# Where the last outputs of the first attention stand among the second's first score rounds, and idle products at two borders

## The reference

```
x = x + attn0(layernorm(x))                  # 16 heads of 64, linear attention, causal, phi = elu + 1
x = x + xattn0(layernorm(x), ctx, mask)      # 16 heads of 16, softmax over 375 context rows, no projections of q, k, v
x = x + ffn0(layernorm(x))                   # own causal attention ("third attention" here), then four experts
x = x + attn1(layernorm(x))                  # causal attention through a rank of 64
x = x + xattn1(layernorm(x), ctx)            # window of 64 rows, rotary
x = x + ffn1(layernorm(x))                   # ternary weights
```

## Time and profile before

| | before |
|---|---|
| median of 3 runs | 1294.95 us |
| profiled execution | 1293.48 us |
| its span, first to last instruction | 1291.7 us |
| mean granted clock of TensorE | 0.991 |
| TensorE busy | 1247.5 us (97%) |
| VectorE busy | 734.2 us (57%) |
| ScalarE busy | 503.1 us (39%) |
| GpSimd busy | 281.4 us (22%) |
| chain that ended last, share on TensorE | 92% |

### The profile page before, as it was taken

How to read it: one execution, slowest core, us unless ns; L and a number is a source line. 1 busy time by engine, 2 the same in 40 slices (tenths; PEclk the granted TensorE clock), 3 DMA queues, 4 the chain that set the end, 5 groups by cost and what they waited for, 6 DMA issues and landing times.

```text
span 1291.7 us, 34601 instructions
## 1 busy us (share of the span) xinstructions
PE 1247.5 (97%) x14031; PEld 969.1 (75%) x14031; DVE 734.2 (57%) x1730; ACT 503.1 (39%) x1075; POOL 281.4 (22%) x382
## 2 busy tenths in 40 slices
PE   7999999999999999899989999999999899999996
PEld 5788777785667666666667999999999677777765
DVE  5666666666666676478764211111112656789987
ACT  2111111120555555556656323323332454444444
POOL 2000000101211111688844000000001000224532
PEclk9999999998999999899999999999999999999999
DMA  7212211101422221012201100000000000000002
GB/s 226 64 45 46 45 31 33 33 20 31 89 68 65 64 61 31 8 48 81 73 16 44 30 1 0 0 3 0 0 1 1 3 7 4 14 19 18 15 11 59
DMA packets 48480, 45.38 MB, mean 35 GB/s; under 512 B 15408, under 2 KB 44896, under 8 KB 48336
## 3 DMA queue, kind: packets, MB, share of 16 engines
q1 hardware_dynamic: 47824, 42.87, 12.7%
q10 hardware_dynamic: 512, 0.46, 0.1%
HBM read 39.44 MB, written 2.78 MB: 33 GB/s over the span
## 4 chain that ended last, share of the span: by engine, by line
PE 92%; issue 2%; DVE 2%; ACT 2%; DMA 1%; SPq 1%; POOL 0%; ACTq 0%; DVEq 0%
PE banks L323 51%; PE banks L831 6%; PE banks L809 4%; PE banks L996 4%; PE banks L316 3%; PE banks L1009 3%; PE banks L847 3%; PE banks L1058 3%; PE banks L970 3%; PE banks L660 2%; PE banks L618 2%; PE banks L1037 2%; ACT area L1571 1%; PE banks L1053 1%; PE banks L900 1%
## 5 line engine op out<-in xcount | busy, mean ns | idle before, releaser
L1856 DVE TENSOR_REDUCE Y_room<-banks 112x2 f32<-112x750 f32 x128 | 114.1, 934 | 46.9 <-PE banks L809 46.7
L2004 DVE TENSOR_REDUCE area<-banks 112x8 f32<-112x896 f32 x96 | 100.1, 1084 | 56.1 <-PE banks L996 56.1
L1571 ACT ACTIVATE area<-banks 112x896 f32<-112x896 f32 x96 | 82.8, 914 | 111.2 <-PE banks L1058 111.2
L323 PE MATMUL banks<-room,area 128*112 128x256 f32 (+1 forms) x384 | 118.9, 460 | 0.3 <-ACT Y_room L1448 0.3
L2136 DVE SCALAR_TENSOR_TENSOR X<-banks,area,X 128x192 f32 (+1 forms) x56 | 23.3, 417 | 160.4 <-PE banks L323 160.2
L1649 ACT ACTIVATE room<-banks 128x256 f32<-128x256 f32 x123 | 47.2, 384 | 166.0 <-PE banks L323 165.9
L323 PE MATMUL banks<-area,room 128*128 128x224 f32 x512 | 102.6, 360 | 0.6 <-ACT area L1415 0.6
L1458 ACT ACTIVATE area<-banks,Y_room 125x896 f32<-125x896 f32 x96 | 90.1, 1010 | 32.1 <-PE banks L831 31.4
L323 PE MATMUL banks<-room,l 128*128 128x256 f32 x448 | 99.5, 379 | 0.0
L323 PEld LDWEIGHTS banks<-area,room 128*128 128x128 f32 x512 | 97.1, 193 | 3.1 <-ACT area L1415 1.0
L1303 POOL TENSOR_TENSOR rstd<-mv,kcol 112x1 f32<-112x1 f32 x48 | 9.5, 197 | 400.3 <-DVE mv L1979 400.3
(11 more groups left out here) (237 smaller groups left out, 2419.2 us busy)
## 6 DMA issues: line engine op xcount, KB each, us to landing
area<-den_scratch SPq DMA_DIRECT2D x32, 224.0 KB, 3.6
Y_room<-in_ctx SPq DMA_DIRECT2D x16, 375.0 KB
area<-in_ctxT SPq DMA_DIRECT2D x64, 93.8 KB
area<-area SPq DMA_DIRECT2D x192, 2.6 KB
l<-in_l SPq DMA_DIRECT2D x2, 1024.0 KB, 5.4
room<-in_ctxT SPq DMA_DIRECT2D x16, 112.0 KB, 2.1
X<-in_x SPq DMA_DIRECT2D x1, 1568.0 KB, 17.8
out<-X SPq DMA_DIRECT2D x12, 112.0 KB, 2.0
```

The costliest lines, as they stand in the source:

```text
L323: last = nc.tensor.matmul(dst, a, w, start=(k == 0), stop=(k == len(lhs) - 1))
L1571: a_.activation(c_pT[:, i * 8 * S:(i + 1) * 8 * S].rearrange("p (j n) -> p j n", j=2), banks[0:S, 2 + 2 * i:4 + 2 * i, 0:4 * S], ACT.Exp). ...
L1856: v_.tensor_reduce(b_nb[u][:, 4 * a + k:4 * a + k + H + 1:H], banks[0:S, 2 * x:2 * x + 2, 0:SC], AX_X, ALU.max, negate=True).then_inc(Bs[" ...
L2004: v_.tensor_reduce(c_nb[:, 8 * i:8 * i + 8].rearrange("q (j n) -> q j n", j=2), banks[0:S, 2 + 2 * i:4 + 2 * i, 0:4 * S].rearrange("q j (n ...
```

## The change

In `bank_pairs()`, round 0 of batch 1 takes the pairs longest unused, as the others do. `output_a` takes a part of its eight products, and for the last batch writes bank 6 instead of bank 7 (`residual_a` reads it there). On TensorE, `weighted_a(15)` stands in front of round 1, `output_a(14)` between rounds 1 and 2, four idle products behind `queries_b(0)`, three behind round 3. The first half of `output_a(15)` and `maxima_t(0)` stand in front of round 0 of batch 1, the second half behind it, without the wait for ScalarE's copy of the maxima. The idle products behind round 2 of batch 0 and rounds 0 and 1 of batch 1 go. On VectorE, `residual_a(14)` and the statistics of batch 2 stand behind the maxima of round 1, `normalised(15)` in front of those of round 3. At the second border idle products stand behind `output_b(14)` (3), `sums_t(15)` (3), `output_t(15)` (2) and `to_columns(0)` (3), all into bank 5.

```diff
--- before.py
+++ after.py
@@ -176,7 +176,7 @@
     for b in range(B + 1):
         for what, n in [("s", n) for n in range(3)] + [("t", n) for n in range(3)] + [("s", 3)] + [("t", n) for n in range(3, 6)]:
             if what == "s" and on(b):
-                x, y = (0, 1) if b == 0 or (b, n) == (1, 0) else sorted(range(3), key=lambda i: since[i])[0:2]
+                x, y = (0, 1) if b == 0 else sorted(range(3), key=lambda i: since[i])[0:2]
                 pairs["s", b, n] = [claim(x, ("nb", 8 * b + 2 * n + 1)), claim(y, ("nb", 8 * b + 2 * n + 2))]
             m = b - 1
             if what == "t" and on(m):
@@ -619,15 +619,20 @@
                                          a_at[:, h * S:(h + 1) * S], start=True, stop=True, tile_position=(0, LD * e))
                 last.then_inc(A["nd"].sem, 1)
 
-            def output_a(b):
-
-                pe.wait_ge(A["nm"].sem, A["nm"].at(2 * b + 2))
-                pe.wait_ge(A["xu"].sem, A["xu"].at(b))
-                pe.wait_ge(A["xte"].sem, A["xte"].at(min(b // 2 + 2, B // 2)))
-                if b == 0:
-                    pe.wait_ge(ld["a3"].sem, 16)
-                products(pb[7][0:S, 0:D], [a_oT[:, m * S:(m + 1) * S] for m in range(8)],
-                         [wo0[:, m, :] for m in range(8)]).then_inc(A["wd"].sem, 1)
+            def output_a(b, lo=0, hi=8):
+
+                if lo == 0:
+                    pe.wait_ge(A["nm"].sem, A["nm"].at(2 * b + 2))
+                    pe.wait_ge(A["xu"].sem, A["xu"].at(b))
+                    pe.wait_ge(A["xte"].sem, A["xte"].at(min(b // 2 + 2, B // 2)))
+                    if b == 0:
+                        pe.wait_ge(ld["a3"].sem, 16)
+                    if b == B - 1:
+                        pe.wait_ge(pre["b6"].sem, 1)
+                for m in range(lo, hi):
+                    last = T3.matmul(pb[6 if b == B - 1 else 7][0:S, 0:D], a_oT[:, m * S:(m + 1) * S], wo0[:, m, :], start=(m == 0), stop=(m == 7))
+                if hi == 8:
+                    last.then_inc(A["wd"].sem, 1)
 
             def phase_a(p):
 
@@ -753,12 +758,13 @@
                 last.then_inc(Bs["ut"].sem, 1)
 
             def phase_b(b, w, quarter):
+                if b == 1:
+                    output_a(B - 1, 0, 4)
+                    maxima_t(0, 0)
                 if on(b):
                     scores_b(b, 0, w, quarter)
                 if b == 1:
-                    maxima_t(0, 0)
-                    pe.wait_ge(Bs["me"].sem, Bs["me"].at(1))
-                    output_a(B - 1)
+                    output_a(B - 1, 4, 8)
                 if on(b - 2):
                     weighted(b - 2, 0, w % 2)
                     weighted(b - 2, 1, w % 2)
@@ -809,10 +815,7 @@
                     last = T3.matmul(pb[2 * x + r % 2][0:S, 0:SC], b_q[w][o:o + HD + 2, k, r % 2, :], b_ctx[w][o:o + HD + 2, k, 0:SC],
                                      start=True, stop=True)
                 last.then_inc(Bs["sg"].sem, 1)
-                if b == 0 and k > 1:
-                    pe.wait_ge(pre["b6"].sem, 1)
-                    keep_busy(6, 3)
-                if b == 1 and k < 2:
+                if (b, k) == (0, 3):
                     keep_busy(6, 3)
 
             def turned(b, n, w):
@@ -857,11 +860,13 @@
             pe.wait_ge(pre["masks"].sem, 1)
             scores_b(0, 0, 0, 0)
             sums_a(B - 1)
-            output_a(B - 2)
             weighted_a(B - 1)
             scores_b(0, 1, 0, 0)
+            output_a(B - 2)
+            scores_b(0, 2, 0, 0)
             queries_b(0)
-            scores_b(0, 2, 0, 0)
+            pe.wait_ge(pre["b6"].sem, 1)
+            keep_busy(6, 4)
             scores_b(0, 3, 0, 0)
             def project_qk(n):
 
@@ -1109,8 +1114,11 @@
                 for t in range(4):
                     weighted(n, t, n % 2)
                 output_b(n - 1)
+                keep_busy(5, 3)
                 sums_t(n)
+                keep_busy(5, 3)
                 output_t(n)
+                keep_busy(5, 2)
                 output_b(n)
                 pe.wait_ge(W["xn"].sem, W["xn"].at(4))
                 pe.wait_ge(W["xte"].sem, W["xte"].at(3))
@@ -1716,7 +1725,7 @@
 
                 dve.wait_ge(A["wd"].sem, A["wd"].at(b + 1))
                 dve.wait_ge(A["xb"].sem, A["xb"].at(b + 1))
-                v_.tensor_tensor(xb_(b), xb_(b), pb[7][0:S, 0:D], ALU.add).then_inc(A["xu"].sem, 1)
+                v_.tensor_tensor(xb_(b), xb_(b), pb[6 if b == B - 1 else 7][0:S, 0:D], ALU.add).then_inc(A["xu"].sem, 1)
 
             def phase_a(p):
                 def masked(i, n):
@@ -1873,17 +1882,17 @@
                 phase_a(p)
             highest(0, 0, 0)
             highest(0, 1, 0)
-            residual_a(B - 2)
             v_.memset(pb[6][:, 0:4 * S], 0.0).then_inc(pre["b6"].sem, 1)
             queries(0)
             highest(0, 2, 0)
             highest(0, 3, 0)
+            stats_of(Bs, 2, 1, 0)
+            residual_a(B - 2)
             highest(0, 4, 0)
             highest(0, 5, 0)
-            stats_of(Bs, 2, 1, 0)
+            normalised(B - 1)
             highest(0, 6, 0)
             highest(0, 7, 0)
-            normalised(B - 1)
 
 
             def rotary(n):
```

## The result

| | before | after |
|---|---|---|
| median | 1294.49 us (1293.68 to 1295.39) | 1287.04 us (1286.36 to 1288.03) |
| ratio | | 0.9943, 95% interval 0.9931 to 0.9955 |
| profiled execution, span | 1293.48, 1291.7 | 1287.50, 1285.7 |
| mean granted clock | 0.991 | 0.998 |

A forecast was written before the change was run, and what follows sets the result against it. TensorE, busy 187.47 of 188.00 us in the second attention, was taken as the bound. Gains of 5.8 + 0.9 = 6.7 us took 1293.48 to 1286.8; with 1.47 for the median, 1288.2, range 1285.8 to 1291.8.

The forecast's parts named there:

- First border, 5.8: Entry to the second attention's batch 1: `residual_a(15)`, which releases the first weights, comes 5.8 us earlier, at 313.4 instead of 319.18.
- The split: First border's 5.8 us divided: 3.1 from the clock level, 2.7 from the new order.
- The step that was called the one that matters: First border, VectorE: `normalised(15)` starts at 306.6 instead of 310.67, no longer behind eight maxima.
- The level holds: Granted clock stays 1.00 through the first border; rival that it falls there gives 1291.3 us, chance 0.15.
- Second border, 0.9: Entry to the third attention: idle products keep the clock, ScalarE begins 0.8 sooner; gain 0.9 us, bounds 0 and 4.1.
- A: First border: time from the sums of batch 15 to the first weights; 28.35 us before, 22.6 forecast.
- The rival of a gain that is eaten: Second attention: a transfer or loop eats the first border's gain; 1293.5 to 1295 us, chance 0.06.
- The rival of idle products that outlast their waits: Second border: clock falls ahead of the idle products, 1.6 us lost, 1290.7; part of a rival with chance 0.12.
- The total: Whole kernel: 6.7 us gained, median 1288.2 us, chance 0.58.

The follow-up runs named there:

- e4: The kernel before with its order kept and seven more idle products at the first border; median 1292.67 us, ratio 0.9980.
- e7: The changed kernel with `normalised(15)` back behind all eight maxima of batch 0 on VectorE; median 1292.95 us, ratio 0.9990 to the kernel before.
- e3: The changed kernel without the seven idle products at the first border; median 1289.26 us, ratio 0.9958 to the kernel before.
- e5: The changed kernel with `output_a(14)` back in front of `weighted_a(15)` and round 1; median 1291.84 us, ratio 0.9978 to the kernel before.
- e6: The changed kernel with `output_a(15)` in one piece before the turning of the maxima and round 0 of batch 1; median 1290.70 us, ratio 0.9970.
- e9: The changed kernel with five idle products behind the value projection of the third attention's first step; median 1287.84 us, ratio 0.9957 to the kernel before.
- e1: The changed kernel without the eleven idle products at the second border, first time; median 1288.48 us, ratio 0.9959 to the kernel before.
- e1b: The changed kernel without the eleven idle products at the second border, a second time; median 1287.89 us, ratio 0.9950 to the kernel before.
- e2: The kernel before with only the eleven idle products at the second border added; median 1295.13 us, ratio 1.0003.
- e8: The changed kernel with twice as many idle products at the second border (6, 6, 4, 6); median 1288.82 us, ratio 0.9961 to the kernel before.
- a1: The changed kernel timed again, unaltered, beside the kernel before; median 1286.32 us, ratio 0.9942.
- c1: The changed kernel with `residual_a(15)` before the queries of batch 2 and two instead of three idle products behind round 3; median 1290.35 us, ratio 0.9970.

## Why the prediction was right

- **First border, 5.8**: 5.98 measured. The path (banks of round 1, `normalised(15)`, second output, residual, clearing, weights) is the one in the trace, with no step off by more than 0.3. The split is shown by e4: 3.30 for the level against 3.1, 2.68 for the order against 2.7. The step that was called the one that matters, the early `normalised(15)`, does matter (e7).
- **The level holds**: in the profile after and its rerun. The prediction gave the outputs and the idle products as reasons. By the mean clocks, a kernel without one of them keeps the level in few executions: 1 of 6 without the idle products (e3), 3 of 12 without the output between the rounds (e5), 2 of 10 without the split (e6).
- **Second border, 0.9**: 0.97 in the profiles, with the loop of GpSimd and VectorE setting the pace (e9); ScalarE's copies begin 0.77 sooner, where 0.8 was forecast. But it was taken as a gain of every execution. Without the idle products the level fell later and for a shorter time in both profiles (e1, e1b), with 0 to 0.45 lost, and e2 has no gain in the median. That the profiled pair shows 0.97 is in part luck.
- **A shift is passed on whole by the second attention**: 187.89 of 188.00 us busy after, and from the first weights to `output_b(14)` it is 212.80 to 212.86 us in eight profiles with A between 22.36 and 28.25. The rival of a gain that is eaten falls.
- **Mis-sized**: an idle product at the full level takes 0.19 to 0.21 from start to start where 0.23 was used. The rival of idle products that outlast their waits added up the excess of each; at the full level such delays don't add (e8), so it was probably priced too high. Its own case, the low level ahead of them, no run shows. Round 2 of batch 1 waits 0.45, not 1.0, for its maximum, which costs nothing either way.
- **The total**: the medians lie 7.45 apart, 0.75 more than forecast and within their scatter. The spans of the two profiles lie 6.0 apart: 6.95 from the two borders, 0.46 from between them and -1.42 from the start and the fourth attention, neither of which the change touches. The runs don't show whether the kernel before had more low stretches on the mean than its profile.

## What to carry to other kernels

At a border between stages, look for the last instruction that releases the next stage and lay out both engines from the first moved instruction on; here a long run of products between short waiting rounds won by hiding a wait (0.66 us in e5) and, by all signs, by keeping the clock. Price an idle product by the level it keeps, and expect that to differ from execution to execution: read several, not one profile. And when an instruction is moved forward, ask what it releases on GpSimd and what VectorE does at that moment.

## What the runs showed of the hardware

- The low level (0.50) falls at other places in other executions of the same kernel: e1 had it for some 3.4 us at the second border once and twice as long the other time; the profile after had it for some 3.4 us between 996 and 1002, the one of its rerun (a1) not there.
- It fell behind waits of 0.53 us and less in the six us ahead in the kernel before (306.5) and in e3 (near 309), and stayed up in the changed kernel over a wait of 1.65 us (543.57).
- A tensor_scalar pair of VectorE took 2.90 (c1) instead of 0.59 us (after) under a memset of GpSimd; four reductions from PSUM took 3.71 with it (after) and 3.70 without (c1).
